# MLP matmuls of two transformer layers as three float32r products of split operands, with weights streamed through a ring

## The chip, the cores and the metric

One core of a Trainium2 chip runs the whole kernel in one launch. The metric is the device time in microseconds (us), the median of several executions. The engines are TensorE (PE, with its weight loads shown apart as PEld), VectorE (DVE), ScalarE (ACT), GpSimd (POOL), and SyncE (SP), whose queue issues every DMA of this kernel.

## The reference

Two layers run one after the other on `x` (2 batches, 1024 tokens, 256 features) and a context of 154 tokens per batch, with 16 heads of 16 features. All numbers are float32.

```python
# layer 0
h = ln(x);  x = x + attn(rope(h wq), rope(h wk), h wv, causal=True) wo
h = ln(x);  x = x + attn(rope(h wq), rope(y wk), y wv, causal=False) wo
h = ln(x);  x = x + gelu_tanh(h @ fc1_w + fc1_b) @ fc2_w + fc2_b        # 256 -> 1024 -> 256
# layer 1: queries from x, keys and values from the context
h = ln(attn(x Wq.T, y Wk.T, y Wv.T, causal mask) + x)
out = gelu(h @ W1.T + b1) @ W2.T + b2 + h                               # 256 -> 1024 -> 256
```

Biases are left out of the attention lines. The two MLPs are what the change touches.

## The kernel before

The 2048 tokens are cut into four chunks of 512 (`c` = 0 to 3; the last is `LAST`). For each chunk the kernel goes through: layer norm and projections (`prologue`), causal self-attention (`sa`), cross-attention of layer 0 (`ca`), MLP of layer 0, cross-attention of layer 1 (`la`), layer norm, MLP of layer 1, store. Every one of these is cut into small steps: `("max", ...)` computes a tile of scores and its row maximum, `("row", ...)` turns the maxima and places them as an extra row of the queries by two DMAs, `("exp", ...)` computes scores again and exponentiates, `("pv", ...)` multiplies with the values, `("place", ...)` scatters a projection's parts by six DMAs, `("stats", ...)` and `("tr", ...)` are a layer norm and its transposes.

An MLP (`mlp(l, c)`) is 8 pairs of steps. `up` m multiplies the chunk's 256 features with 128 of the 1024 hidden columns: two matmuls of 512 columns into the one bank `ps_misc`. ScalarE applies gelu from there into `hid` (two slots). `down` m multiplies this piece with 128 rows of the second weight: four matmuls of 256 columns which are summed over all 8 pairs in the two banks `ps_exp`. `res` adds the sums to the residual. The order is up 0, up 1, down 0, up 2, down 1, and so on. There are 8 MLPs, so 64 pairs. All MLP weights lie in SBUF as `w_up` and `w_down` (4 MB in all): those of layer 0 are loaded at the start, those of layer 1 at the step `late`.

The order of all steps is one list, `ORDER`. `order()` makes it with a planner at build time: ten threads of steps, a table `COST` of assumed durations, and priorities; it takes at each turn the step that could start on the PE first. Each engine then walks the same list and does its part of every step, in order. Since the sums of an MLP occupy `ps_exp`, the planner lets no `exp` step stand between the first `up` and the `res` of an MLP; `max` steps may stand there. Since every engine is in order, a wait in one step holds up all later steps of that engine. GpSimd has little to do: the third part of each projection (L1248), eight instructions per chunk for the output of the last layer norm (`lnout`, L1255), and some setup.

The steps of the prediction are in these places: `up` and `down` on PE at L835 and L852, gelu at L1191, `max` at L889 and L891 on PE and at L1114 on DVE, the SP queue at L622 to L709.

## Time and profile before

| | |
|---|---|
| median of 3 runs | 1119.23 us |
| lowest, highest | 1112.74, 1123.27 us |
| span of the profiled execution | 1118.3 us |
| PE busy | 936.4 us (84%) |
| DVE busy | 582.5 us (52%) |
| ACT busy | 419.9 us (38%) |
| POOL busy | 73.3 us (7%) |
| HBM read, written | 13.32 MB, 2.10 MB |

The profiled execution has a span of 1118.3 us from its first to its last instruction. No time of its own is given beside that; the span is 0.9 us under the median of the runs. Busy times are unions of the records. A PE record contains the drain of the array, so two matmuls that follow each other overlap in the records, and the spacing of their starts is what a matmul costs in a stream.

### The profile page before, as it was taken

What the parts mean: (1) busy time and instruction counts of PE and PEld (TensorE: products, weight loads), DVE (VectorE), ACT (ScalarE), POOL (GpSimd) and SP (SyncE); (2) the same over time, 40 slices, a digit from 0 to 9 for tenths busy, and PEclk for the clock granted to TensorE, in tenths of its full rate; (3) what the DMA queues carried; (4) which work ended last, traced back from release to release, by engine and by line L of the source; (5) the groups of instructions that cost most, each with busy time, mean ns of one, the idle gap of its engine ahead of it and who ended that gap; (6) DMA issues with size and microseconds to landing.
All of it is one profiled execution on the core that took longest, in us unless ns stands there. A gap on an engine that the chain in (4) does not pass through costs nothing.

```text
span 1118.3 us, 13782 instructions
## 1 busy us (share of the span) xinstructions
PE 936.4 (84%) x5180; PEld 456.9 (41%) x5180; DVE 582.5 (52%) x1347; ACT 419.9 (38%) x822; POOL 73.3 (7%) x83
## 2 busy tenths in 40 slices
PE   3888864899988898888989867999887888987898
PEld 1433322345443353434445324633233454442365
DVE  5555637784667704488545675665125504415500
ACT  1133331342355625353422431167763323343421
POOL 2102000000000200000000001000000000000210
PEclk9988886799999999988999897999998999998999
DMA  7805462202132100645020401013004004022000
GB/s 275 102 1 73 75 139 43 24 2 27 23 38 30 29 1 20 94 51 66 1 30 1 57 13 17 10 40 48 1 20 57 2 1 57 2 37 22 1 19 19
DMA packets 47013, 43.85 MB, mean 39 GB/s; under 512 B 13510, under 2 KB 44386, under 8 KB 46434
## 3 DMA queue, kind: packets, MB, share of 16 engines
q1 hardware_dynamic: 46948, 42.98, 24.0%
q8 instruction: 42, 0.69, 0.3%
q14 instruction: 23, 0.19, 0.1%
HBM read 13.32 MB, written 2.10 MB: 14 GB/s over the span
## 4 chain that ended last, share of the span: by engine, by line
PE 57%; DVE 17%; DMA 10%; ACT 8%; SPq 5%; issue 4%; ACTq 0%; DVEq 0%
PE ps_exp L852 10%; PE ps_o L964 10%; PE ps_misc L835 10%; PE ps_max L889 8%; ACT probs L1200 5%; DVE mcol L1114 5%; SPq L695 4%; PE ps_exp L922 4%; DMA QA<-part 4%; PE ps_chain L814 3%; PE ps_chain L822 3%; DVE swap L1028 2%; DMA QC<-part 2%; PE ps_exp L927 2%; PE ps_chain L787 2%
## 5 line engine op out<-in xcount | busy, mean ns | idle before, releaser
L1114 DVE TENSOR_REDUCE mcol<-ps_max 128x3 f32<-128x462 f32 (+5 forms) x496 | 292.2, 626 | 181.9 <-PE ps_max L891 106.1
L1200 ACT ACTIVATE probs<-ps_exp 128x512 f32<-128x512 f32 (+3 forms) x544 | 261.1, 523 | 242.0 <-PE ps_exp L925 87.0
L889 PE MATMUL ps_max<-KA,QA 96*128 96x512 bf16 (+3 forms) x384 | 117.9, 359 | 55.3 <-DVE mcol L1114 24.4
L922 PE MATMUL ps_exp<-QA,KA 98*128 98x512 bf16 (+3 forms) x384 | 120.4, 350 | 26.1 <-ACT probs L1200 18.3
L835 PE MATMUL ps_misc<-hT,w_up 128*128 128x512 f32 x256 | 125.7, 615 | 7.2 <-ACT hid L1191 2.2
L852 PE MATMUL ps_exp<-w_down,hid 128*128 128x256 f32 x512 | 128.2, 388 | 0.0
L1191 ACT ACTIVATE hid<-ps_misc,col 128x512 f32<-128x512 f32 x64 | 44.0, 687 | 200.4 <-PE ps_misc L835 200.4
L852 PEld LDWEIGHTS ps_exp<-w_down,hid 128*128 128x128 f32 x512 | 94.5, 190 | 29.7 <-issue 15.5
L1248 POOL TENSOR_TENSOR part<-rot,part 128x512 bf16<-128x512 f32 (+1 forms) x36 | 40.8, 1133 | 923.2 <-DVE part L1038 923.2
L889 PEld LDWEIGHTS ps_max<-KA,QA 96*128 96x128 bf16 x384 | 39.2, 104 | 123.1 <-DVE mcol L1114 63.6
L964 PE MATMUL ps_o<-probs,V 128*17 128x512 f32 (+3 forms) x768 | 85.1, 517 | 3.2 <-ACT probs L1200 2.3
L922 PEld LDWEIGHTS ps_exp<-QA,KA 98*128 98x128 bf16 x384 | 36.9, 101 | 115.4 <-ACT probs L1200 88.5
L1028 DVE TENSOR_TENSOR swap<-rot,sinT 64x512 f32<-64x512 f32 (+1 forms) x56 | 36.9, 659 | 59.0 <-ACT rot L1173 48.2
L835 PEld LDWEIGHTS ps_misc<-hT,w_up 128*128 128x128 f32 x256 | 47.9, 195 | 47.3 <-issue 41.3
L891 PE MATMUL ps_max<-mask,idb 128*128 128x128 bf16 (+1 forms) x320 | 65.8, 234 | 0.0
L889 PE MATMUL ps_max<-KC,QC 96*128 96x154 bf16 x384 | 53.1, 255 | 10.3 <-DMA QC<-part 5.1
L925 PE MATMUL ps_exp<-mask,idb 128*128 128x128 bf16 x256 | 56.9, 234 | 0.0
L1054 DVE TENSOR_TENSOR xb<-xb,ps_exp 128x512 f32<-128x512 f32 x16 | 10.6, 682 | 85.3 <-PE ps_exp L852 85.3
L1173 ACT ACTIVATE rot<-ps_chain,col 128x512 f32<-128x512 f32 (+1 forms) x36 | 24.1, 668 | 76.1 <-PE ps_chain L814 68.1
L889 PEld LDWEIGHTS ps_max<-KC,QC 96*128 96x128 bf16 x384 | 32.3, 106 | 41.8 <-DVE mcol L1114 24.1
L1157 ACT ACTIVATE hT<-ps_chain,col 128x256 f32<-128x256 f32 x64 | 31.3, 565 | 48.0 <-PE ps_chain L787 47.9
L964 PE MATMUL ps_o<-probs,VA 128*17 128x512 f32 x256 | 36.7, 647 | 14.0 <-ACT osb L1207 13.5
(109 smaller groups left out, 986.6 us busy)
## 6 DMA issues: line engine op xcount, KB each, us to landing
QA<-part SPq DMA_DIRECT2D x72, 128.0 KB, 5.1
QC<-part SPq DMA_DIRECT2D x72, 128.0 KB, 5.2
KA<-part SPq DMA_DIRECT2D x48, 128.0 KB, 5.2
xb<-in_x SPq DMA_DIRECT2D x8, 512.0 KB, 6.1
out<-xb SPq DMA_DIRECT2D x4, 512.0 KB, 3.0
KC<-part SPq DMA_DIRECT2D x24, 77.0 KB, 3.1
w_up<-in_fc SPq DMA_DIRECT2D x1, 1024.0 KB, 7.0
w_down<-in_fc SPq DMA_DIRECT2D x1, 1024.0 KB, 8.2
```

What stands on the lines that cost most here:

```text
L695: sp.dma_start(dst, part[:, n % 2, i, :]).then_inc(s_put[key][f], 16)
L835: mm = pe.matmul(bank[:, :], w_up[l][:, t, m * P:(m + 1) * P], hT_of("up", c)[:, t, :], start=(t == 0), stop=(t == KT - 1))
L852: mm = pe.matmul(dst, hid[:, m % 2, t * P:(t + 1) * P], w_down[l][:, m, :], start=False, stop=(m == NM - 1), skip_group_check=True)
L889: mm = pe.matmul(dst, q, kk, start=True, stop=not causal)
L891: mm = pe.matmul(bank[:, at0 + a0:at0 + a0 + w0], idb[:, :], mk, start=False, stop=True)
L922: mm = pe.matmul(bank[:, q0:CH], KA[:, g // NT, hh, (g % NT) * P:(g % NT + 1) * P], QA[:, hh, q0:CH], start=True, stop=(r < 0))
L925: mm = pe.matmul(bank[:, q0:q0 + P], idb[:, :], maskt, start=False, stop=True)
L964: mm = pe.matmul(ps_o[p0:p0 + HD + 1, q0:CH], v, pr, start=first, stop=last, skip_group_check=True)
L1028: ins = dve.tensor_tensor(w[lo:lo + 64, a0:a0 + wd], r[hi:hi + 64, a0:a0 + wd], sinT[hi:hi + 64, t0:t0 + wd], ALU.mult)
L1114: dve.tensor_reduce(dst, src, AX.X, ALU.max).then_inc(s_max_done, 1)
L1191: act.activation(hid[:, m % 2, :], ps_misc[:, :], (ACT.Gelu_apprx_tanh, ACT.Gelu)[l], bias=c0(("fc1_b", "l1_b1")[l], m)).then_inc(s_misc_f ...
L1200: act.activation(probs[:, n % 2, h, q0:CH], ps_exp[exp_nth[s] % 2][:, q0:CH], ACT.Exp).then_inc(s_exp_done, 1)
```

## The change

Each operand of the MLP matmuls is split into a rounded part and the rest (high and low), and each product is made of three matmuls in the type float32r: high with low, low with high, high with high (`PRODUCTS`). So `up` has six matmuls of 512 columns in place of two in float32, and `down` has twelve of 256 columns in place of four.

**Weights.** At the start 16 `split` steps bring one pair's weights (256 KB) each into `stage`, GpSimd rounds them and subtracts (two instructions), and SP writes both parts (512 KB) to a scratch in DRAM. A step `refill` then loads the first six pairs into the ring `wm`, and each `down` is followed by the load of the pair six further on. The 4 MB of resident weights are gone.

**Activations.** After the transposes of ln3 and ln4 come two `round` steps: DVE rounds half of the chunk into `hTr`, GpSimd computes the rest. After each gelu DVE copies `hidf` to `hidh` rounded, and GpSimd writes the rest to `hidl`; `down` waits for that. These buffers lie in the memory of `probs`, so the gelu of the first pair waits for all earlier `pv` steps, and the planner starts an MLP only when none is open.

**Order.** The table `COST` is changed and the planner places everything anew. The places that the prediction speaks of follow.

PE in the MLP of layer 1 for chunk 1, third and fourth pair. Names: `w_up`, `w_down` are the weights before, `wm` the ring, `ps_max` the score tiles. Before:

```order
L835 MATMUL ps_misc<-hT,w_up 128x512 x2
L889 MATMUL ps_max<-KA,QA 128x512 x2
L852 MATMUL ps_exp<-w_down,hid 128x256 x4
L889 MATMUL ps_max<-KA,QA 128x512
L891 MATMUL ps_max<-mask,idb 128x128
L889 MATMUL ps_max<-KA,QA 128x512
L891 MATMUL ps_max<-mask,idb 128x128
L835 MATMUL ps_misc<-hT,w_up 128x512 x2
```

Now:

```order
L994 MATMUL ps_misc<-idf,mcol 16x128
L921 MATMUL ps_misc<-hTr,wm 128x512 x6
L941 MATMUL ps_exp<-wm,hidh 128x256
L941 MATMUL ps_exp<-wm,hidl 128x256
L941 MATMUL ps_exp<-wm,hidh 128x256 x2
L941 MATMUL ps_exp<-wm,hidl 128x256
```

Most `max` steps have left this MLP. It had 34 between its first `up` and its `res` and has 5; over the 8 MLPs the number falls from 99 to 60 (20, 4, 27, 34, 6, 8, 0, 0 before in the order in which they run; 22, 6, 13, 5, 0, 14, 0, 0 now).

GpSimd at the end of the program, last two MLPs of layer 1. Before, `lnout` was all that stood there:

```order
L1255 TENSOR_TENSOR xb<-a_ctx,g4b 128x256 x4
L1255 TENSOR_TENSOR xb<-xb,g4b 128x256 x4
L1255 TENSOR_TENSOR xb<-a_sa,g4b 128x256 x4
L1255 TENSOR_TENSOR xb<-xb,g4b 128x256 x4
L444 UNCONDITIONAL_BRANCH
```

Now:

```order
L1380 TENSOR_TENSOR hTr<-hT,hTr 128x2x256 x2
L1387 TENSOR_TENSOR xb<-a_sa,g4b 128x256 x4
L1387 TENSOR_TENSOR xb<-xb,g4b 128x256 x4
L1374 TENSOR_TENSOR hidl<-hidf,hidh 128x512 x8
L1380 TENSOR_TENSOR hTr<-hT,hTr 128x2x256 x2
L1387 TENSOR_TENSOR xb<-a_ctx,g4b 128x256 x4
L1387 TENSOR_TENSOR xb<-xb,g4b 128x256 x4
L1374 TENSOR_TENSOR hidl<-hidf,hidh 128x512 x8
```

The eight instructions of `lnout` stand before the first rest of the hidden piece (`hidl`), and the rounding of the second MLP's input stands behind the last `hidl` of the first. Chunk 3 now goes before chunk 2 here.

SP after the first projections. Before, the row of the first four heads was next:

```order
L695 DMA QA<-part 16x8x512 x6
L695 DMA KA<-part 16x8x512 x12
L658 DMA xb<-in_x 128x4x256
L702 DMA QA<-mrow 1x16x128 x4
L695 DMA QA<-part 16x8x512 x6
```

Now:

```order
L783 DMA QA<-part 16x8x512 x6
L783 DMA KA<-part 16x8x512 x12
L727 DMA xb<-in_x 128x4x256
L740 DMA split_w<-wm 128x1024
L744 DMA stage<-in_mlpw 128x512
```

Eight such pairs of a scratch write and a stage load (the first is shown) stand before the first row, four more before the second, and three more before the next projection is placed. On GpSimd the two instructions of each split stand after the first three projection parts.

The diff, cut to its core:

```diff
+PRODUCTS = ((0, 1), (1, 0), (0, 0))
...
+NWM = 6
+WSTEP = KT * P + E
+SPLIT_SLOTS = 4
...
+def rounded(name, c):
+    s = norm(name, c)
+    return s[:3] + [("round", name, c, 0)] + s[3:] + [("round", name, c, 1)]
...
-    return (post_norm("sa", "ln2", c) + cross("ca", c) + out_norm("ca", "ln3", c)
+    return (post_norm("sa", "ln2", c) + cross("ca", c) + out_norm("ca", "ln3", c)[:-2] + rounded("ln3", c)[2:]
             + mlp(0, c) + [("tr", "x3", c, g) for g in range(NT // 2)] + cross("la", c)
-            + [("addatt", c, g) for g in range(NT // 2)] + norm("ln4", c) + [("lnout", c)] + mlp(1, c)
+            + [("addatt", c, g) for g in range(NT // 2)] + rounded("ln4", c) + [("lnout", c)] + mlp(1, c)
...
+def splits():
+    return [("split", l, m) for l in (1, 0) for m in range(NM)] + [("refill",)]
...
-    "up": (("pe", 1.8), ("act", 0.6)), "down": (("pe", 1.78),), "res": (("dve", 0.65),),
+    "up": (("pe", 1.32), ("act", 0.65), ("dve", 0.4), ("pool", 1.15)), "down": (("pe", 1.35),),
+    "round": (("dve", 0.4), ("pool", 1.15)), "split": (("pool", 2.3), ("dma", 1.3)), "res": (("dve", 0.65),),
...
+            w += [("round", ("ln3", "ln4")[s[1]], s[2], g) for g in range(NT // 2)]
+            w.append(("refill",))
...
+        if holder not in (None, i) and k == "round":
+            return None
+        if k == "up" and s[3] == 0 and (part_group or len(pvs) < exp_groups):
...
+        stage = alias("stage", [P, 2, WSTEP], F32, addr["hTr"], 0)
+        hidf = alias("hidf", [P, 2, CH], F32, addr["probs"], 0)
+        hidh = alias("hidh", [P, 3, CH], F32R, addr["probs"], 2 * CH * 4)
+        hidl = alias("hidl", [P, 3, CH], F32R, addr["probs"], 5 * CH * 4)
...
+        def after_down(eng, n):
+            l, m = divmod(n, NM)
+            if m == NM - 1:
+                eng.wait_ge(s_sum_ready, (l + 1) * NT // 2)
+            else:
+                eng.wait_ge(s_down, l * (NM - 1) + m + 1)
...
+                elif k == "split":
+                    _, l, m = s
+                    n = nth[s] - 1
+                    sp.wait_ge(s_split, n + 1)
+                    sp.dma_start(split_w[l * NM + m], wm[:, n % SPLIT_SLOTS, :, :].rearrange("p a n -> p (a n)").bitcast(F32)
+                                 ).then_inc(s_wput[n % SPLIT_SLOTS], 16)
+                    if n + 2 < len(SPLITS):
+                        l, m = SPLITS[n + 2][1:]
+                        sp.dma_start(stage[:, n % 2, :], mlpw[l * NM + m]).then_inc(s_stage[n % 2], 16)
...
+                elif k == "refill":
                     after_chain(sp, ("ctxk", 1, KT - 1))
-                    sp.dma_start(w_up[1][:, :, :], fcw[2]).then_inc(s_wlate, 16)
-                    sp.dma_start(w_down[1][:, :, :], fcw[3]).then_inc(s_wlate, 16)
+                    for i in range(SPLIT_SLOTS):
+                        sp.wait_ge(s_wput[i], 16 * len(SPLITS) // SPLIT_SLOTS)
+                    for n in range(NWM):
+                        _, l, _, m = ups[n]
+                        sp.dma_start(wm[:, n, :, :].rearrange("p a n -> p (a n)").bitcast(F32), split_w[l * NM + m]
+                                     ).then_inc(s_wload[n], 16)
+                elif k == "down" and nth[s] - 1 + NWM < len(ups):
+                    n = nth[s] - 1 + NWM
+                    _, l, _, m = ups[n]
+                    after_down(sp, n - NWM)
+                    sp.dma_start(wm[:, n % NWM, :, :].rearrange("p a n -> p (a n)").bitcast(F32), split_w[l * NM + m]
+                                 ).then_inc(s_wload[n % NWM], 16)
...
                 elif k == "up":
                     _, l, c, m = s
-                    for g in range(NT // 2):
-                        after_chain(pe, ("tr", ("ln3", "ln4")[l], c, g))
-                    if l:
-                        once("wlate", s_wlate, 32)
-                    elif m == 0:
-                        once("wrest", s_wrest, 16 * 7)
+                    n = nth[s] - 1
+                    pe.wait_ge(s_round, nth[("round", ("ln3", "ln4")[l], c, NT // 2 - 1)])
+                    pe.wait_ge(s_wload[n % NWM], 16 * (n // NWM + 1))
                     bank = misc_bank(s)
-                    for t in range(KT):
-                        mm = pe.matmul(bank[:, :], w_up[l][:, t, m * P:(m + 1) * P], hT_of("up", c)[:, t, :],
-                                       start=(t == 0), stop=(t == KT - 1))
+                    for i, (a, b) in enumerate(PRODUCTS):
+                        for t in range(KT):
+                            mm = pe.matmul(bank[:, :], wm[:, n % NWM, a, t * P:(t + 1) * P], hTr[:, b, t, :],
+                                           start=(i == 0 and t == 0), stop=(i == 2 and t == KT - 1))
                     mm.then_inc(s_misc_ready, 1)
...
-                    after_misc(pe, ("up", l, c, m))
+                    n = nth[s] - 1
+                    pe.wait_ge(s_hl, n + 1)
                     for t in range(NT):
                         dst = ps_exp[t // 2][:, (t % 2) * E:(t % 2 + 1) * E]
                         if m == 0:
                             add_bias(dst, ("fc2_b", "l1_b2")[l], start=(t % 2 == 0))
-                        mm = pe.matmul(dst, hid[:, m % 2, t * P:(t + 1) * P], w_down[l][:, m, :],
-                                       start=False, stop=(m == NM - 1), skip_group_check=True)
+                        for i, (a, b) in enumerate(PRODUCTS):
+                            hid = (hidh, hidl)[a]
+                            mm = pe.matmul(dst, hid[:, n % 3, t * P:(t + 1) * P], wm[:, n % NWM, b, KT * P:WSTEP],
+                                           start=False, stop=(m == NM - 1 and i == 2), skip_group_check=True)
                         if m == NM - 1 and t % 2:
                             mm.then_inc(s_sum_ready, 1)
+                        elif m < NM - 1 and t == NT - 1:
+                            mm.then_inc(s_down, 1)
...
+                elif k == "up":
+                    n = nth[s] - 1
+                    after_misc(dve, s)
+                    if n >= 3:
+                        after_down(dve, n - 3)
+                    dve.tensor_copy(hidh[:, n % 3, :], hidf[:, n % 2, :]).then_inc(s_hh, 1)
+                elif k == "round":
+                    _, what, c, g = s
+                    n = (nth[s] - 1) // 2
+                    after_chain(dve, ("tr", what, c, g))
+                    if n == 0:
+                        dve.wait_ge(s_split, len(SPLITS))
+                    else:
+                        dve.wait_ge(s_misc_ready, misc_use[ups[n * NM - 1]] + 1)
+                    dve.tensor_copy(hTr[:, 0, :, 2 * g * P:(2 * g + 2) * P],
+                                    hT_of(what, c)[:, :, 2 * g * P:(2 * g + 2) * P]).then_inc(s_rh, 1)
...
                     act.wait_ge(s_misc_ready, misc_use[s] + 1)
-                    act.activation(hid[:, m % 2, :], ps_misc[:, :], (ACT.Gelu_apprx_tanh, ACT.Gelu)[l],
+                    n = nth[s] - 1
+                    if m == 0:
+                        act.wait_ge(s_pv, pvs_before[s])
+                    if n >= 2:
+                        act.wait_ge(s_hl, n - 1)
+                    act.activation(hidf[:, n % 2, :], ps_misc[:, :], (ACT.Gelu_apprx_tanh, ACT.Gelu)[l],
...
+                elif k == "split":
+                    n = nth[s] - 1
+                    i = n % SPLIT_SLOTS
+                    pool.wait_ge(s_stage[n % 2], 16 * (n // 2 + 1))
+                    if n >= SPLIT_SLOTS:
+                        pool.wait_ge(s_wput[i], 16 * (n // SPLIT_SLOTS))
+                    link(pool.tensor_copy(wm[:, i, 0, :], stage[:, n % 2, :]))
+                    pool.tensor_tensor(wm[:, i, 1, :], stage[:, n % 2, :], wm[:, i, 0, :].bitcast(F32),
+                                       ALU.subtract).then_inc(s_split, 1)
+                elif k == "up":
+                    n = nth[s] - 1
+                    pool.wait_ge(s_hh, n + 1)
+                    pool.tensor_tensor(hidl[:, n % 3, :], hidf[:, n % 2, :], hidh[:, n % 3, :].bitcast(F32),
+                                       ALU.subtract).then_inc(s_hl, 1)
+                elif k == "round":
+                    _, what, c, g = s
+                    pool.wait_ge(s_rh, nth[s])
+                    tok = slice(2 * g * P, (2 * g + 2) * P)
+                    pool.tensor_tensor(hTr[:, 1, :, tok], hT_of(what, c)[:, :, tok],
+                                       hTr[:, 0, :, tok].bitcast(F32), ALU.subtract).then_inc(s_round, 1)
```

## Rows read from the trace of the kernel before

**Rows 1.** The page: busy tenths and granted clock in 40 slices of the span.

```profile
PE   3888864899988898888989867999887888987898
DVE  5555637784667704488545675665125504415500
PEclk9988886799999999988999897999998999998999
```

**Rows 2.** The chain that ended last: its share of the span by line.

```profile
PE ps_exp L852 10%; PE ps_o L964 10%; PE ps_misc L835 10%; PE ps_max L889 8%; ACT probs L1200 5%; DVE mcol L1114 5%; SPq L695 4%; PE ps_exp L922 4%; DMA QA<-part 4%; PE ps_chain L814 3%; PE ps_chain L822 3%; DVE swap L1028 2%; DMA QC<-part 2%; PE ps_exp L927 2%; PE ps_chain L787 2%
```

**Rows 3.** Stretches cut at the MLPs (from, to, length, busy by engine, clock, DMA).

```profile
core 0: us, PE busy (x) PEld busy (x) DVE busy (x) ACT busy (x) POOL busy (x), PEclk, DMA share, GB/s
...
390.60:424.50 33.90, 32.27 (x122) 19.14 (x120) 4.38 (x9) 7.32 (x11) 1.29 (x2) 1.00 0.00 1
...
606.40:681.50 75.10, 55.49 (x368) 25.80 (x369) 53.71 (x119) 28.41 (x58) 8.32 (x10) 0.85 0.27 33
681.50:725.20 43.70, 42.48 (x176) 24.98 (x174) 23.83 (x42) 6.59 (x10) 1.06 (x2) 0.95 0.00 1
...
1049.40:1114.90 65.50, 62.10 (x212) 37.94 (x212) 9.95 (x32) 14.63 (x22) 6.17 (x9) 0.97 0.03 9
```

**Rows 4.** Timeline, one pair without other work: start, length, engine, line, count.

```profile
1071.63 1.88 PE L835 MATMUL ps_misc<-hT,w_up 128*128 128x512 f32 x4
...
1073.35 1.89 PE L852 MATMUL ps_exp<-w_down,hid 128*128 128x256 f32 x8
...
1073.55 0.69 ACT L1191 ACTIVATE hid<-ps_misc,col 128x512 f32<-128x512 f32 x1 [2.76 <-PE ps_misc L835]
...
1075.08 0.59 PE L835 MATMUL ps_misc<-hT,w_up 128*128 128x512 f32 x1
```

**Rows 5.** Timeline of PE: float32 transposes of 128 columns between other matmuls.

```profile
1063.87 1.04 PE L787 MATMUL ps_chain<-idf,a_sa 128*128 128x128 f32 x8
1064.74 0.59 PE L835 MATMUL ps_misc<-hT,w_up 128*128 128x512 f32 x1
```

**Rows 6.** Timeline of an MLP with score tiles between its steps.

```profile
697.36 0.60 PE L889 MATMUL ps_max<-KA,QA 96*128 96x512 bf16 x2
697.78 1.29 DVE L1114 TENSOR_REDUCE mcol<-ps_max 128x1 f32<-128x512 f32 x2 [1.20 <-PE ps_max L889]
697.80 1.88 PE L835 MATMUL ps_misc<-hT,w_up 128*128 128x512 f32 x4
```

**Rows 7.** Groups by form: operations like those that are added.

```profile
L1035 DVE CAST part<-rot 128x512 bf16<-128x512 f32 x32 | 13.7, 427 | 27.2 <-ACT rot L1173 26.4
L1248 POOL TENSOR_TENSOR part<-rot,part 128x512 bf16<-128x512 f32 x32 | 37.7, 1179 | 896.2 <-DVE part L1038 896.2
L1255 POOL TENSOR_TENSOR xb<-xb,g4b 128x256 f32<-128x256 f32 x16 | 11.1, 724 | 0.3
L1222 POOL TENSOR_SCALAR w_ca_wq<-w_ca_wq 128x512 f32<-128x512 f32 x1 | 1.5, 1503 | 0.1
L1114 DVE TENSOR_REDUCE mcol<-ps_max 128x1 f32<-128x512 f32 x192 | 125.9, 685 | 87.1 <-PE ps_max L891 48.3 <-PE ps_max L889 38.0
```

**Rows 8.** Timeline at the end: `lnout` on GpSimd, then the last additions and the store.

```profile
1060.77 2.77 POOL L1255 TENSOR_TENSOR xb<-a_sa,g4b 128x256 f32<-128x256 f32 x4 [10.76 <-DVE a_sa L1096]
...
1063.62 2.78 POOL L1255 TENSOR_TENSOR xb<-xb,g4b 128x256 f32<-128x256 f32 x4
...
1113.31 0.69 DVE L1054 TENSOR_TENSOR xb<-xb,ps_exp 128x512 f32<-128x512 f32 x1 [28.74 <-PE ps_exp L852]
1114.18 0.69 DVE L1054 TENSOR_TENSOR xb<-xb,ps_exp 128x512 f32<-128x512 f32 x1 [0.18 <-PE ps_exp L852]
```

**Rows 9.** Timeline of the start: SP's queue, GpSimd's third projection part.

```profile
39.90 1.15 POOL L1248 TENSOR_TENSOR part<-rot,part 128x512 bf16<-128x512 f32 x1 [5.79 <-DVE part L1038]
42.51 0.60 SPq L658 DMA_DIRECT2D xb<-in_x  x1
67.28 11.80 SPq L702 DMA_DIRECT2D QA<-mrow  x4
83.03 3.81 SPq L695 DMA_DIRECT2D QA<-part  x6
```

**Rows 10.** Timeline: who waited at 91.6 and at 169.5 us.

```profile
91.61 0.23 PE L889 MATMUL ps_max<-KA,QA 96*128 96x128 bf16 x1 [0.20 <-DMA QA<-part]
...
169.50 0.69 DVE L1054 TENSOR_TENSOR xb<-xb,ps_chain 128x512 f32<-128x512 f32 x1 [13.14 <-DMA xb<-in_x]
```

**Rows 11.** DMA issues: count, size of one, median us from issue to landing.

```profile
QA<-part SPq DMA_DIRECT2D x72, 128.0 KB, 5.1
...
xb<-in_x SPq DMA_DIRECT2D x8, 512.0 KB, 6.1
out<-xb SPq DMA_DIRECT2D x4, 512.0 KB, 3.0
...
w_up<-in_l1w SPq DMA_DIRECT2D x1, 1024.0 KB, 5.5
...
w_ca_wo<-in_ca_wo SPq DMA_DIRECT2D x1, 256.0 KB, 3.9
```

92 lines of the change are left out of this document (65 added, 27 removed).

## The prediction, made before the changed kernel ran

> **What bounds the kernel now.** I read the page first. PE is 80 to 90% busy in nearly every slice, DVE up to 80% in the first half and idle in stretches of the second [rows 1]. The chain that ended last has L835 and L852, the MLP matmuls, with 10% of the span each [rows 2]. 20% of 1118.3 us is 224 us, and 64 pairs of an `up` and a `down` at 3.45 us each (below) are 221 us: so the whole matmul stream of the MLPs lies on the chain, and a shorter stream can shorten the run.
>
> The stretches say how the MLPs run [rows 3]. The MLP of layer 1 for chunk 0 takes 33.9 us with PE busy 32.3 and the clock at 1.00: PE alone is its limit. The one for chunk 1 takes 43.7 us with 42.5 of PE, because 34 score tiles stand in it; DVE has 23.8 us there and follows easily. The last two take 65.5 us with nothing else to run. The stretch before the MLP of chunk 1 is another kind: 75.1 us with only 55.5 of PE and 53.7 of DVE. Outside the MLPs PE waits for others.
>
> **The stream.** In a bare pair the first `up` record starts at 1071.63, the first `down` at 1073.35, the next `up` at 1075.08 [rows 4]: 1.72 us for `up`, 1.73 for `down`, 3.45 together. One float32 matmul is two records; four records of 512 columns take 1.72, so one matmul takes 0.86. A bfloat16 matmul of 512 columns takes 0.22 (two records in 0.60 with the second one's drain of 0.38) [rows 6]. No row has float32r. The bounds of its price are these two, 0.22 and 0.86, a factor of four apart with no value between them in any row. I take the lower one for streaming: float32's price is four times bfloat16's to the percent, which looks like four products of half-width parts, and a type whose operand is one rounded part has one. The Trainium skill, FP8 and Floating Point Precision, section TensorE Precision Notes, says this of the array: true float32 takes four passes, and reduced float32 is read and cut to its native width, which makes one. By that page the sum would be the same as mine.
>
> `up` is then 6 x 0.216 = 1.30 us. In `down` each matmul has new weights of 4 bytes and only 256 columns (0.11). The nearest row is the eight float32 transposes: each loads 128 new columns and streams 128, and they take 1064.74 - 1063.87 = 0.87, 0.109 each [rows 5], twice what 128 columns stream in. So a load costs about 0.11 and lies beside the stream. With 256 columns both are 0.11, and `down` is 12 x 0.11 = 1.32. A pair is 2.62 in place of 3.45, and 64 pairs give **-53 us**. If loads did not overlap, this would be otherwise (rival 3).
>
> **The chain inside a pair.** `down` m used to need gelu m. Now it needs gelu, a DVE copy and a GpSimd subtraction. Counted from the next PE record after `up` m: 0.20 to the start of gelu, 0.69 gelu [rows 4], 0.43 the copy (CAST, 427 ns), about 1.25 the subtraction (1179 ns with one bfloat16 operand; two float32 operands of 256 take 724) [rows 7], and some 0.27 for three handovers: **L = 2.8 us**. Meanwhile PE has `down` m-1 and `up` m+1, 2.62 us. Where L is the longer, each second step waits and a pair settles at (L + 2.62)/2 = 2.71. Score tiles between steps cover this, so it costs 0.09 in the 32 pairs of chunks 2 and 3 at most: **+2**. With a row maximum (0.69 us, [rows 7]) ahead of the copy, L is 3.5 and the price 14.
>
> **Start and end of each MLP.** `down` 0 has only `up` 1 (1.30) before it, so PE waits 1.5; `down` 7 has only `down` 6, again 1.5. Before, gelu was shorter than either. 3 us in about four MLPs without cover: **+12**. Before `up` 0 come the two `round` steps, of which the second is exposed: 0.43 on DVE and 1.25 on GpSimd and handovers, 2 us in four MLPs: **+8**. In the last pair of MLPs this is worst. The second one's rounding waits on DVE for the `res` steps of the first and then runs twice on GpSimd, about 4 us in which PE has nothing; and `lnout`, 5.6 us of GpSimd [rows 8], stands between the rounding and the first `hidl`, so that `down` 0 comes at 5.6 + 1.3 after `up` 0 starts in place of 4.1. That is 2.8 for each of the two: **+6**. The 4 us are in the +8. So the last two MLPs, 65.5 us now, gain hardly anything: -13 in the stream, +6 for ends, +6 for rounding and +6 for `lnout`.
>
> **The start.** GpSimd begins the splits after its third projection part, at 41.1 us [rows 9]. One split is a copy and a subtraction; no row has a float32 copy there, and a TENSOR_SCALAR of the size took 1.50, a TENSOR_TENSOR 1.18 [rows 7], so one split is 2.4 to 2.9. `stage` has two slots: split n+2 needs the load that SP issues after the write of split n. 0.5 us for issuing the write, then 3.9 us to landing (256 KB with others ahead) [rows 11], then 2.6 for the split: 7.1 for two, 3.55 each, unless the 512 KB write ahead (3.0, as the store) adds itself, then 5. Split 8 ends at 43.7 + 7 x 3.55 = 68.5, against 67.28 when SP issues the first row [rows 9]: nearly nothing. SP passes the 15th at 93.4 and only then places the next projection, which started at 83.03. PE took up the first tile that needs it at 91.61 with 0.20 us of waiting [rows 9, 10], so a placement 10 to 12 us later is felt. The planner put some 3 us of other steps ahead: **+8**, with 0 and +27 (5 us a split) as ends.
>
> Against this stands a wait that goes. The reload of `xb` was issued at 159.38 and used at 169.50, after 13.14 us of idle DVE [rows 10], behind 2 MB of layer-1 weights; its median is 6.1 [rows 11]. Now the ring's 3 MB come behind it: **-5**, at most -6.
>
> **The placing of score tiles.** 39 of the 99 tiles leave the MLPs. In there each cost PE 0.22 to 0.28; outside it costs DVE 0.69 [rows 7]. Where PE waits anyway the move gives back 39 x 0.28 = 11 us; where DVE is the limit, as in the 75.1 us before the MLP of chunk 1 [rows 3], it costs 39 x (0.65 - 0.28) = 14. Both occur: the MLP of chunk 1 goes from 43.7 to about 26 us, and the stretch before it grows by its tiles. I take **-3**.
>
> **More work for DVE and DMA.** 64 copies and 16 roundings are 80 x 0.43 = 34 us of DVE, nearly all in MLPs where it has half its time free; I cost them at nothing beyond L. That cover is thin where a projection's rope (four or five instructions of 0.4 to 0.7 us) stands ahead of a copy; five projections now lie inside MLPs and one did. DMA carries 40 MB more (4 in, 8 out, 32 back, less 4 of old loads). A pair's 512 KB every 2.7 us is 190 GB/s, and the ring is six pairs deep, 16 us, so no `up` should wait for it. But SP is one queue and its placements (5.1 us each, [rows 11]) now queue behind 512 KB loads: **+3** for both, 0 to +10.
>
> **Sum.** -53 + 2 + 12 + 8 + 6 + 8 - 5 - 3 + 3 = -22 us against the profiled 1118.3: 1096. The median of the runs is 0.9 above that span, so the forecast is **1097 us**.
>
> **Rivals.**
>
> 1. *The stream's gain comes nearly whole.* The ends are covered by other chunks' steps, the moved tiles fall where PE waits (-11), the start costs nothing. -53 + 0 + 6 + 5 + 4 + 0 - 5 - 11 + 2 = -52: 1067 us. For it: PE is busy 55.5 of 75.1 us in [rows 3], so there is room. Against it: the last two MLPs have no cover.
>
> 2. *The chain through three engines becomes the bound* (slower). A pair costs (L + 2.62)/2. The other terms add up to +29, without the +2 for L. So if all 64 pairs run at L, the run is no faster from 3.45 - 29/64 = 3.0 us a pair on, which is L = 3.4, about what one row maximum ahead of the copy gives. At L = 3.9 (a maximum and a slow subtraction) a pair is 3.26: -12 + 29 = +17, 1136 us. For it: DVE and GpSimd are in order and DVE's maxima stand between `up` steps. Against it: the tiles that delay the copy also fill PE.
>
> 3. *Weight loads do not overlap with the matmuls of float32r* (slower). Then each of the 18 matmuls of a pair costs 0.11 more: 2.62 + 2.0 = 4.6 us, 64 x 1.15 = +74, with the others 1220 us. The trace speaks against it: the transposes run at 0.109, where 0.107 for the load and 0.053 for the stream would be 0.16 one after the other [rows 5]. The Trainium skill, TensorE: Matmul & The Clock Gate, Part 3, The mechanism, says that weight loads overlap with matmuls in flight only where the row group differs, which would make this rival true; here float32 loads of the same rows overlap, and the measurement decides.
>
> 4. *The start eats the rest.* At 5 us a split the projection comes 27 us late, and the sum is -3: 1116 us, no change.
>
> **How the numbers follow.** A difference of 1% (11 us) is what a measurement of this kernel can tell. The forecast (1080 to 1112) gets 0.50, rival 1 0.15, rival 2 0.15, rival 3 0.03, rival 4 and mixtures near zero 0.17. Faster, under 1108: nearly all of the forecast's case (0.45) and rival 1, 0.60. Within 1%: the rest of the forecast's case and rival 4, 0.21. Slower: rivals 2 and 3, 0.18, and a little of 4, 0.19. The range of 8 in 10 runs from rival 1's end with 4 us more, 1063, to rival 2's 1136.
>
> **What would show it.** L921 and L941 records starting 0.216 and 0.11 apart (wrong if 0.21 for L941). In the last MLP a pair every 2.7 us; a higher value gives L. PE idle 4 us between the last two MLPs, and some 3 more before the first `down` after `lnout`. SP's first `QA<-mrow` near 69 us and the next `QA<-part` near 94. The wait for `xb<-in_x` near 160 us shrinking to about 3. The MLP of chunk 1, layer 1, at 26 us. The forecast is wrong if the stretches between MLPs grow together by more than 20 us, or if `up` waits for the ring.

## The result: 3.5% slower, and the profile after

The changed kernel takes 1157.03 us (median of 4 runs, 1154.93 to 1158.85), the kernel before beside it 1117.68 (4 runs): a ratio of 1.035, 95% interval 1.030 to 1.039. The forecast was 1097, faster; the time lies outside the range of 1063 to 1136. The profiled execution spans 1157.1 us against 1118.3, so 39 us are to be found.

The page of the changed kernel first: PE and its granted clock in 40 slices, the chain that ended last, and the groups that answer to [rows 1, 2, 7] (busy us, mean ns | idle before, releaser).

```profile
PE   3886875898998977989878786979896898876678
PEclk9897777799999988999989697989997799979588
...
PE ps_o L1055 10%; PE ps_exp L941 7%; PE ps_max L980 6%; PE ps_misc L921 6%; DVE mcol L1221 5%; ACT probs L1312 4%; PE ps_exp L1013 4%; SPq L783 4%; PE ps_chain L902 3%; PE ps_chain L910 3%; DMA QC<-part 3%; DMA QA<-part 2%; DMA stage<-in_mlpw 2%; PE ps_exp L1018 2%; PE ps_chain L875 2%
...
L921 PE MATMUL ps_misc<-hTr,wm 128*128 128x512 f32 x384 | 113.4, 435 | 17.0 <-POOL hTr L1380 12.6
L941 PE MATMUL ps_exp<-wm,hidh 128*128 128x256 f32 x512 | 117.5, 304 | 11.7 <-POOL hidl L1374 11.7
...
L1374 POOL TENSOR_TENSOR hidl<-hidf,hidh 128x512 fp32r<-128x512 f32 x64 | 82.4, 1289 | 170.6 <-DVE hidh L1151 170.6
...
L1151 DVE CAST hidh<-hidf 128x512 fp32r<-128x512 f32 x64 | 31.9, 500 | 146.0 <-ACT hidf L1303 145.9
...
wm<-split_w SPq DMA_DIRECT2D x64, 512.0 KB, 3.3
```

The stream did shrink: L921 and L941 hold 13% of the chain where L835 and L852 held 20% [rows 2]. What is new is idle PE with GpSimd's name on it, 12.6 us before `up` and 11.7 before `down` (3.7 more stand before the bias matmuls that open `down` 0), and a lower clock: 0.89 on average against 0.93. PE is busy 935.7 us, as before (936.4), though its stream is shorter. The ring is no bound; no group of PE names `wm<-split_w`. The eight MLPs together take 278.2 us against 283.6, so all the rest of the program has grown by 44 us.

A bare pair, late in the MLP that runs last but one (start, length, line, count), as [rows 4]:

```profile
1098.38 1.55 PE L921 MATMUL ps_misc<-hTr,wm 128*128 128x512 f32 x6
1099.76 0.34 PE L941 MATMUL ps_exp<-wm,hidh 128*128 128x256 f32 x1
...
1101.25 1.55 PE L921 MATMUL ps_misc<-hTr,wm 128*128 128x512 f32 x6
```

`up` takes 1.38 (six matmuls, 0.23 each), `down` 1.49 (twelve, 0.12 each), a pair 2.87, and 2.82 to 2.87 elsewhere. A float32 matmul of 512 columns took 0.86 [rows 4], so this one costs little over a quarter, and the load of its 4-byte weights is hidden. So rival 3 is dead. The Trainium skill, TensorE: Matmul & The Clock Gate, Part 3, The mechanism, says in its list that loads overlap with matmuls in flight only when the row group differs, though its text also names a background weight buffer as a second way; here they overlap on the same rows, `down` at 0.12 a matmul. The Trainium skill, FP8 and Floating Point Precision, TensorE Precision Notes, gives float32 four passes and reduced float32 a read that is cut to the native width; the trace agrees with one pass for it. But 2.85 is not 2.62.

The end of the run, the changed kernel's stretches from the last step of attention on: from, to, length, then busy time of each engine, clock, DMA.

```profile
1065.80:1082.50 16.70, 3.10 (x13) 2.30 (x13) 12.81 (x54) 4.24 (x7) 2.66 (x3) 0.61 0.00 0
1082.50:1115.60 33.10, 30.69 (x150) 24.40 (x151) 4.46 (x9) 5.51 (x8) 15.87 (x16) 0.78 0.34 112
1119.70:1153.00 33.30, 29.97 (x148) 23.61 (x148) 4.91 (x10) 5.51 (x8) 15.88 (x16) 0.80 0.10 35
```

For 16.7 us PE has 3.1 us of work, while DVE does 12.8: two chunks are normalized one behind the other. Then two MLPs take 33 us each at a clock of 0.78 and 0.80, where the bare MLP of the kernel before took 30.4 at 1.00. Three things stand there in one place: an order, waits at the edges, and half clock behind them. The chain shows the edge (start, length, what):

```profile
1079.84 2.60 POOL hTr L1380 x2
1082.43 2.77 POOL xb L1387 x4
1085.27 2.96 POOL xb L1387 x4
1088.23 1.24 POOL hidl L1374
...
1094.69 2.42 PE ps_misc L921 x6
```

Rounding, then all of `lnout`, then the rest of the first gelu, all on GpSimd, before the first `down`; and an `up` at 1094.69 that takes 2.42 us for the six matmuls that take 1.39 a pair later: the granted clock was still 0.5 until 1096.8, while PE had its work again from 1089.6 on.

### The profile page after: what moved, and what is told of

Same layout as the page of the kernel before. It is cut to its first block, busy times and chain, and to the rows that moved or that the text cites. A ratio compares the mean times of both kernels' runs of the same rounds, so it can differ in the third digit from the quotient of the medians.

```text
span 1157.1 us, 14983 instructions
## 1 busy us (share of the span) xinstructions
PE 935.7 (81%) x5564; PEld 489.9 (42%) x5564; DVE 624.7 (54%) x1427; ACT 419.1 (36%) x820; POOL 207.2 (18%) x195
## 4 chain that ended last, share of the span: by engine, by line
PE 49%; DVE 18%; DMA 11%; ACT 7%; POOL 5%; SPq 5%; issue 4%; POOLq 0%; DVEq 0%; ACTq 0%
PE ps_o L1055 10%; PE ps_exp L941 7%; PE ps_max L980 6%; PE ps_misc L921 6%; DVE mcol L1221 5%; ACT probs L1312 4%; PE ps_exp L1013 4%; SPq L783 4%; PE ps_chain L902 3%; PE ps_chain L910 3%; DMA QC<-part 3%; DMA QA<-part 2%; DMA stage<-in_mlpw 2%; PE ps_exp L1018 2%; PE ps_chain L875 2%
## 5 line engine op out<-in xcount | busy, mean ns | idle before, releaser
L1221 DVE TENSOR_REDUCE mcol<-ps_max 128x1 f32<-128x512 f32 (+5 forms) x496 | 291.0, 625 | 102.5 <-PE ps_max L982 54.0
L980 PE MATMUL ps_max<-KA,QA 96*128 96x512 bf16 (+3 forms) x384 | 119.9, 360 | 48.1 <-DVE mcol L1221 34.8
L1013 PE MATMUL ps_exp<-QA,KA 98*128 98x512 bf16 (+3 forms) x384 | 119.4, 347 | 26.8 <-ACT probs L1312 18.8
L921 PE MATMUL ps_misc<-hTr,wm 128*128 128x512 f32 x384 | 113.4, 435 | 17.0 <-POOL hTr L1380 12.6
L941 PE MATMUL ps_exp<-wm,hidh 128*128 128x256 f32 x512 | 117.5, 304 | 11.7 <-POOL hidl L1374 11.7
L1374 POOL TENSOR_TENSOR hidl<-hidf,hidh 128x512 fp32r<-128x512 f32 x64 | 82.4, 1289 | 170.6 <-DVE hidh L1151 170.6
L1303 ACT ACTIVATE hidf<-ps_misc,col 128x512 f32<-128x512 f32 x64 | 44.1, 689 | 186.5 <-PE ps_misc L921 186.5
L1151 DVE CAST hidh<-hidf 128x512 fp32r<-128x512 f32 x64 | 31.9, 500 | 146.0 <-ACT hidf L1303 145.9
L941 PEld LDWEIGHTS ps_exp<-wm,hidh 128*128 128x128 f32 x512 | 88.8, 197 | 24.5 <-POOL hidl L1374 18.2
L921 PEld LDWEIGHTS ps_misc<-hTr,wm 128*128 128x128 f32 x384 | 74.6, 206 | 38.0 <-POOL hTr L1380 13.7
L980 PEld LDWEIGHTS ps_max<-KA,QA 96*128 96x128 bf16 x384 | 37.4, 101 | 125.8 <-DVE mcol L1221 91.9
L1380 POOL TENSOR_TENSOR hTr<-hT,hTr 128x512 fp32r<-128x512 f32 x16 | 20.3, 1272 | 310.0 <-DVE hTr L1160 310.0
L941 PE MATMUL ps_exp<-wm,hidl 128*128 128x256 f32 x256 | 74.1, 289 | 0.0
L980 PE MATMUL ps_max<-KC,QC 96*128 96x154 bf16 x384 | 54.2, 258 | 11.0 <-DMA QC<-part 6.4
```

Source lines behind the costliest of these rows:

```text
L921: mm = pe.matmul(bank[:, :], wm[:, n % NWM, a, t * P:(t + 1) * P], hTr[:, b, t, :], start=(i == 0 and t == 0), stop=(i == 2 and t == KT - 1))
L941: mm = pe.matmul(dst, hid[:, n % 3, t * P:(t + 1) * P], wm[:, n % NWM, b, KT * P:WSTEP], start=False, stop=(m == NM - 1 and i == 2), skip_ ...
L980: mm = pe.matmul(dst, q, kk, start=True, stop=not causal)
L1013: mm = pe.matmul(bank[:, q0:CH], KA[:, g // NT, hh, (g % NT) * P:(g % NT + 1) * P], QA[:, hh, q0:CH], start=True, stop=(r < 0))
L1221: dve.tensor_reduce(dst, src, AX.X, ALU.max).then_inc(s_max_done, 1)
L1303: act.activation(hidf[:, n % 2, :], ps_misc[:, :], (ACT.Gelu_apprx_tanh, ACT.Gelu)[l], bias=c0(("fc1_b", "l1_b1")[l], m)).then_inc(s_misc_ ...
```

## The experiments

Ratios are to the kernel before, run beside each on the same chip (its medians 1117.7 to 1123.7); 0.001 is 1.1 us. In the names, `own` means that the hidden tiles have memory of their own, with a ring of four pairs; `before` and `rule` mean the order of the kernel before, as it is or with the planner's rule on open score groups. lnout_spread, one_split, no_rest and the names with `after` keep the changed kernel's order, after_tail up to its last 174 steps.

```
                          ratio    95% interval       median us
changed kernel            1.0346   1.0301 to 1.0391   1157.0
order_rule_on_f32         0.9831   0.9796 to 0.9866   1103.4
own_hid                   1.0095   1.0055 to 1.0134   1134.7
lnout_spread              1.0274   1.0230 to 1.0318   1152.3
one_split                 1.0199   1.0160 to 1.0239   1144.0
f32_after_order           1.0261   1.0230 to 1.0292   1150.5
own_before_order          1.0162   1.0114 to 1.0210   1138.3
own_rule_order_spread     1.0020   0.9991 to 1.0049   1122.7
no_rest                   1.0092   1.0061 to 1.0124   1131.9
after_tail                1.0231   1.0193 to 1.0269   1146.7
after_warm                1.0291   1.0253 to 1.0329   1153.5
after_dve                 1.0319   1.0281 to 1.0358   1155.8
own_rule_dve              1.0178   1.0133 to 1.0222   1139.8
own_before_no_rest        0.9905   0.9868 to 0.9942   1108.5
own_before_one_product    0.9756   0.9706 to 0.9807   1092.2
f32r_one                  0.8907   0.8851 to 0.8964    996.4
f32r_one_cost             0.9147   0.9076 to 0.9217   1024.2
```

### Four suspects, one alone each

My theory was O, the order: the hidden tiles now lie in the score tiles' memory, and the planner may open an MLP only when no score group is open. Rivals: P, the work at the MLPs' edges (later called W); S, the splits at the start.

```diff
 (order_rule_on_f32: to the planner of the kernel before)
+        if k == "up" and s[3] == 0 and (part_group or len(pvs) < exp_groups):
+            return None
 (own_hid: to the changed kernel)
-NWM = 6
+NWM = 4
-        hidf = alias("hidf", [P, 2, CH], F32, addr["probs"], 0)
+        hid_ = sb("hid", [P, 6, CH])
+        hidf = alias("hidf", [P, 2, CH], F32, addr["hid"], 0)
-        if k == "up" and s[3] == 0 and (part_group or len(pvs) < exp_groups):
-            return None
 (lnout_spread: GpSimd, behind each hidl subtraction of layer 1)
+                        ins = pool.tensor_tensor(x_of(c)[:, t, :], ..., g4b4[:, i, :], (ALU.mult, ALU.add)[i])
 (one_split)
-SPLITS = splits()[:-1]
+SPLITS = splits()[:1]
```

> The kernel before (float32 matmuls, weights resident, gelu tiles of their own) with one rule added to its planner: up 0 of an MLP is not taken while a score group or a pv is open. Theory O (the order is the cause): this rule alone costs most of the loss; the planner's own clock gives 20 to 30 us, so 1138 to 1148 us. Theory P (the third engine in the chain and the work at the edges of the MLPs is the cause): the order costs little, 1113 to 1125 us. Theory S (the splits at the start): the same 1113 to 1125.

> The changed kernel with the MLP's hidden tiles in 12 KB of their own in place of the score tiles' memory, hidh and hidl two deep, the ring four pairs deep in place of six to make room, and the planner's rule on open groups taken out. Theory O: 20 to 30 us come back, 1127 to 1137 us. Theory P: nearly nothing, 1150 to 1158 us. If the ring of four runs dry, up waits for wm and the time does not fall, whatever the order.

> The changed kernel with the eight multiply and add instructions of lnout spread over the MLP, one behind each hidl subtraction, in place of all eight ahead of the first one; the order is the same. Theory P: down 0 comes some 3.5 us earlier in the last two MLPs and up to as much in the two others of layer 1, 7 to 14 us: 1143 to 1150 us. Theory O or S: 1153 to 1157 us.

> The changed kernel with one weight step split in place of sixteen; every load of the ring reads that one step, so the output is not the reference's, and the order is the same. Theory S: the start stretch gets 15 us or more shorter, 1140 us or less. Theories O and P: about 7 us, what the start stretch lost at equal progress of PE (248 us before, 255 after at a fifth of its other work), 1147 to 1153 us.

The first fell clean outside every expectation: with the rule, the float32 kernel is 1.7% **faster**. So the rule is not what costs, and theory O in that form is dead. What is left is stranger: two orders of the same float32 work differ by 19 us, and the planner's own clock, its end of the last step, had them the other way round (1014.7 us for the old, 1017.8 with the rule). own_hid gained 2.5%, in a third order, so by itself it proves nothing on memory. lnout_spread gained 0.7%, 8 us, as expected of the edges; its interval overlaps that of the changed kernel, though the traces differ by 7.5 us too. one_split gained 1.5%, 16 us, more than P allowed and less than S asked: 11 of it are there at a fifth of PE's other work (244.1 us against 255.2).

### Order and work taken apart

The next pair completes a square: old work in the new order, and new work in the old order.

```diff
 (f32_after_order: the kernel before, planned by the changed kernel's planner)
+def order():
+    return [s for s in order_all() if s[0] not in ("split", "refill", "round")]
 (own_before_order: own_hid, planned by the planner of before, new steps put in)
+    for s in order_f32():
+        out.append(s)
+        out += [t for a, t in zip(ANCHORS, SPLITS) if a == s]
+        if s[0] == "tr" and s[1] in ("ln3", "ln4"):
+            held.append(("round", *s[1:]))
+        if s[0] == "up":
+            busy = s[3] < NM - 1
+        if not busy:
+            out += held
+            held = []
```

> The kernel before (float32 matmuls, resident weights, gelu tiles of their own) with the changed kernel's order of all steps, without its split, round and refill steps. It gives the price of the order alone. Theory O (the order is the cause): 15 to 35 us over before, 1138 to 1158 us. Theory W (the work at the MLPs' edges is the cause, and the low clock behind it): within 10 us of before, 1113 to 1133 us.

> The changed kernel's work (three float32r products, splits, ring of four, hidden tiles in their own memory) with the order of the kernel before, the split, round and refill steps put in at the nearest places. It gives the price of the work alone at the old order. Theory O: the stream's 38 to 53 us mostly show, 1075 to 1095 us. Theory W: the edges give the stream back, 1115 to 1135 us.

Both theories hold half. **The order alone costs 2.6%**, 29 us, with not one instruction changed. **The work alone costs 1.6%** at the old order, 18 us, where its stream should have saved 38. Their sum, 4.2%, is near the 3.5% of both together. The square is not quite closed: own_before_order has memory of its own for the hidden tiles and a ring of four, the changed kernel shares memory and has six. That sharing was not run alone; but the changed kernel is only 0.8% over f32_after_order, so it is not what costs most. Neither half of the planner's change makes a slow order by itself: the rule with the old table `COST` gave 0.983, and the new table and steps without the rule gave own_hid's order (1.0095, against 1.0162 for the same work in the old order). The slow order has both.

Where the order loses is read at points where PE has started the same share of its other work (4412 matmul records outside the MLPs in both traces) and has done the same MLPs: f32_after_order is 7 us behind at 45% (489.2 us against 482.5), 20 behind at 70%, 13 at 95%, 28 at the end. So half of it lies in the tail, where the last head of chunk 2 is scored after all of chunk 3. The old order normalizes chunk 3 on DVE inside the MLP of chunk 2, as this row of the kernel before shows; that MLP began at 1049.4:

```profile
1059.31 1.38 DVE L1096 TENSOR_SCALAR a_sa<-xb,mv,nw 128x256 f32<-128x256 f32 x4
```

In the new order the same work stands on the chain (f32_after_order: start, length, what, up to the first `up`, which float32 too has to wait for):

```profile
1063.11 1.32 DVE st L1106 x4
...
1070.41 1.42 DVE st L1106 x4
...
1077.38 1.11 PE ps_chain L823 x4
1078.49 3.43 PE ps_misc L871 x4
```

PE's waits tell a part of the rest. Its waits for normalized rows (`a_ctx`), first in the kernel before, then in f32_after_order (us in total, times, longest):

```profile
PE ps_chain L787 <- DVE a_ctx L1096: 6.7, 2, 6.1
PE ps_chain L823 <- DVE a_ctx L1132: 25.5, 7, 7.4
```

Only the 7.4 of it, and 5.8 for the other chunk's rows (`a_sa`), lie in the tail; the other six are spread over the run. The waits for `mcol` grew from 31.6 to 42.3 us, those for placed queries (`QA<-part`) fell from 30.7 to 19.3.

The work is read from the MLPs alone. The sum line gives the length of the eight together, then each engine's busy time; first the kernel before, then own_before_order, whose MLPs hold the same steps in the same order.

```profile
1049.40:1083.90 34.50, 32.73 (x113) 20.08 (x114) 7.90 (x30) 9.13 (x14) 6.17 (x9) 0.95 0.00 0
1083.70:1114.10 30.40, 29.53 (x101) 18.04 (x99) 1.39 (x3) 5.50 (x8) 0.00 (x0) 1.00 0.05 18
sum 283.60, PE 272.30 PEld 164.36 DVE 81.56 ACT 55.93 POOL 10.73; mean PE 34.04 PEld 20.54 DVE 10.19 ACT 6.99 POOL 1.34
```

```profile
583.70:621.40 37.70, 35.77 (x196) 26.34 (x196) 18.76 (x34) 5.51 (x8) 10.18 (x8) 0.90 0.35 100
...
894.50:926.70 32.20, 29.36 (x166) 23.43 (x166) 8.27 (x20) 5.51 (x8) 10.22 (x8) 0.89 0.34 116
...
1063.30:1100.80 37.50, 29.77 (x160) 24.33 (x160) 14.88 (x39) 7.33 (x12) 24.25 (x26) 0.91 0.29 99
1101.80:1129.10 27.30, 25.10 (x148) 20.54 (x148) 4.10 (x9) 5.51 (x8) 10.30 (x8) 1.00 0.36 116
sum 280.10, PE 250.19 PEld 194.89 DVE 106.56 ACT 46.58 POOL 108.33; mean PE 31.27 PEld 24.36 DVE 13.32 ACT 5.82 POOL 13.54
```

64 pairs at 0.6 us less should have made 284 into 245; it is 280. PE's busy time fell by 22 us, not by 38, and its idle time in the MLPs grew from 11.3 us (283.6 less 272.3) to 29.9. The last MLP alone, without cover and at full clock, gained 3.1 us (27.3 against 30.4) of 4.8. The other seven had clocks of 0.89 to 0.96, where before five of the eight had 1.00.

The rest of the work's loss lies outside, 18 us. The start is 8.3 us longer (261.3 against 253.0, as forecast). And once, ahead of the MLP at 583.7, the rounding stood behind a projection's rotation on DVE and GpSimd; PE waited 7.51 us for it:

```profile
583.71 1.22 PE L918 MATMUL ps_misc<-hTr,wm 128*128 128x512 f32 x2 [7.51 <-POOL hTr L1375]
```

```profile
579.27 0.43 DVE L1126 CAST part<-rot 128x512 bf16<-128x512 f32 x1
579.61 1.71 DVE L1157 CAST hTr<-hT 128x512 fp32r<-128x512 f32 x2
...
581.00 2.66 POOL L1375 TENSOR_TENSOR hTr<-hT,hTr 128x512 fp32r<-128x512 f32 x2
```

### The third engine, and what a wait costs

no_rest and own_before_no_rest leave out the two GpSimd subtractions, in the new and the old order.

```diff
-                    pe.wait_ge(s_hl, n + 1)
+                    pe.wait_ge(s_hh, n + 1)
-                            hid = (hidh, hidl)[a]
+                            hid = hidh
 (and hTr[:, 0] for hTr[:, b], no subtraction behind "up" and "round" on GpSimd)
```

> The changed kernel in its own order, without the GpSimd subtractions behind the gelu and behind the rounding of h: the rounded part stands in the products in place of the rest, as many matmuls as before, so the output lacks the rests' share. Theory W: the chain of three engines costs 1.3 us at either end of eight MLPs, 1.3 to 2.6 in the rounding, up to 3.5 of lnout in some (lnout no longer stands ahead of what down 0 waits for), and the low clock behind the waits: 25 to 45 us, 1115 to 1135 us. Theory O: under 12 us, 1148 us or more.

> own_before_order (the changed work in the order of the kernel before, 1.6% over it) without the two GpSimd subtractions; the rounded part stands in the products in place of the rest, as many matmuls as before. Its eight MLPs take 280 us in the trace where the stream alone would have made 284 into 246. Theory W (the waits for the third engine at the MLPs' edges, and the half clock behind them, give the stream back): 20 to 30 us come back, 0.990 to 0.998 of before, 1108 to 1118 us. If the split at the start and DVE's extra work are what counts: less than 8 us, 1.010 or more.

Both bring back 2.5 to 2.6% (1.0346 to 1.0092, 1.0162 to 0.9905), 29 us, with as many matmuls. That holds the waits, the half clock behind them, and `lnout`, which then no longer stands ahead of `down` 0. The eight MLPs of own_before_no_rest:

```profile
886.50:914.90 28.40, 26.39 (x166) 22.13 (x166) 8.87 (x21) 6.24 (x9) 0.00 (x0) 1.00 0.37 116
...
1076.70:1102.30 25.60, 24.70 (x150) 20.93 (x148) 4.98 (x11) 5.51 (x8) 0.00 (x0) 1.00 0.44 142
sum 258.70, PE 242.35 PEld 191.80 DVE 106.19 ACT 50.00 POOL 7.57; mean PE 30.29 PEld 23.97 DVE 13.27 ACT 6.25 POOL 0.95
```

21.4 of the trace's 26.8 us (1133.2 less 1106.4) come out of the MLPs. The last one is now 25.6 us: eight pairs at 2.85 and 2.8 for its two ends. The one at 886.5 went from 32.2 to 28.4 and its clock from 0.89 to 1.00: with the wait the low clock is gone too. 258.7 is still 13 over 245; the DVE copy is still in the chain, and one of these MLPs ran at a clock of 0.80.

after_warm prices that clock: the changed kernel with matmuls of nothing in PE's waits around the last two MLPs.

```diff
+WARM = {("turn", "la", 2, 3): 20, ("tr", "ln4", 3, 1): 18, ("tr", "ln4", 2, 0): 9, ("up", 1, 3, 1): 15,
+        ("tr", "ln4", 2, 1): 12, ("up", 1, 2, 1): 14}
+                    for _ in range(WARM[s[1]]):
+                        pe.matmul(ps_max[0][:, :], idb[:, :], mask[:, 0:512], start=True, stop=True)
```

> The changed kernel with 88 matmuls of nothing (bfloat16, 512 columns, into a bank that nobody reads) at six places where PE waits before and in the last two MLPs. Theory C (after a wait PE runs at half clock, and that is part of the price): the 14.3 and 13.7 us of low clock inside these MLPs go, 8 to 14 us less than the changed kernel, about 1145 us. Without it (only the waits themselves cost): no change, or 1 to 3 us more, since the matmuls can stand in the way.

```profile
1070.40:1087.20 16.80, 12.05 (x59) 5.65 (x58) 12.83 (x54) 4.24 (x7) 2.69 (x3) 1.00 0.01 1
1087.20:1117.50 30.30, 28.31 (x165) 22.16 (x166) 4.83 (x9) 5.51 (x8) 15.88 (x16) 1.00 0.35 122
1121.60:1151.70 30.10, 28.11 (x162) 21.83 (x162) 4.81 (x9) 5.51 (x8) 15.88 (x16) 1.00 0.11 39
```

Same waits, same order, clock 1.00 in place of 0.61, 0.78 and 0.80: the two MLPs take 30.3 and 30.1 us in place of 33.1 and 33.3. In the traces that is 6.0 us, less than the 8 to 14 expected, and less than half of the 14 that 28.0 us at half clock could cost; the traces as a whole differ by only 1.3 us, since this one was already 4.6 behind at the first filler matmul. The ratio went down by 0.006, also 6 us, but the two intervals overlap, so by the runs alone it would be open. The Trainium skill, TensorE: Matmul & The Clock Gate, HAM oscillation — how this bites in real kernels, says that a wait throttles PE and the work behind it starts at half clock; the trace agrees.

own_before_one_product keeps everything but two of the three products.

```diff
-PRODUCTS = ((0, 1), (1, 0), (0, 0))
+PRODUCTS = ((0, 0),)
```

> own_before_order with one float32r product in place of three, all copies, subtractions, splits and ring loads kept; the output lacks the rests' share. PE's part of a pair falls from 2.85 to 0.95 us. If PE's stream still set the pace of the MLPs: 64 times 1.9, 120 us less. By the chain (gelu, copy, subtraction and handovers, 2.8 us) a pair settles at (2.8 + 0.95)/2 = 1.9 us: 64 times 0.95, 60 us less where nothing else covers, less some for more half clock and for MLPs with score tiles in them: 40 to 65 us less, 1073 to 1100 us.

```profile
1061.30:1083.40 22.10, 15.87 (x52) 9.22 (x52) 3.85 (x9) 5.50 (x8) 10.16 (x8) 0.73 0.42 139
sum 228.40, PE 169.21 PEld 100.14 DVE 106.42 ACT 46.45 POOL 107.19; mean PE 21.15 PEld 12.52 DVE 13.30 ACT 5.81 POOL 13.40
```

Two thirds of the stream gone, 122 us, and the run gains 4.1%, 46 us, within the 40 to 65 expected. The pair itself is slower than the 1.9 us expected, 2.1 over four pairs of this last MLP at full clock, where `down` waits for the subtraction:

```profile
1072.05 0.73 PE L938 MATMUL ps_exp<-wm,hidh 128*128 128x256 f32 x4 [0.53 <-POOL hidl L1369]
...
1080.56 0.74 PE L938 MATMUL ps_exp<-wm,hidh 128*128 128x256 f32 x4 [1.01 <-POOL hidl L1369]
```

So with three products PE's stream (2.85) and the chain of gelu, copy and subtraction (2.8) are of one size, and little of a shorter stream comes through: 46 us of 122.

### Repairs

after_tail gives the changed kernel the old order for its last 174 steps; after_dve and own_rule_dve put the subtractions on DVE; own_rule_order_spread has the order of order_rule_on_f32 and `lnout` spread as above.

```diff
 (after_tail)
+    o = o[:o.index(("res", 0, 3, 1)) + 1]
+    return o + [tuple(...) for s in TAIL.split()]
 (after_dve, own_rule_dve)
+                    dve.wait_ge(s_hh, n + 1)
+                    dve.tensor_tensor(hidl[:, n % 3, :], hidf[:, n % 2, :], hidh[:, n % 3, :].bitcast(F32),
+                                      ALU.subtract).then_inc(s_hl, 1)
```

> The changed kernel with the last 174 steps (all behind the second layer-0 MLP of the last two chunks) in the order that the kernel before has them in; the round steps stand behind their transposes. The last head of chunk 2 is then scored before chunk 3's, so that one chunk's last normalization runs on DVE beside work of PE. Theory O (half of the order's loss sits in this tail: 28.5 us at the end against 13.7 at 95% of PE's other work): 10 to 18 us less than the changed kernel, 2.1 to 2.6% over before, 1143 to 1150 us. If the tail's place in the order is not what costs: within 5 us of the changed kernel.

> The changed kernel with both subtractions (hidl, and the rest of h) on DVE behind the rounding copies, in place of GpSimd. An instruction should take 0.65 us in place of 1.29, one handover less, and lnout no longer stands ahead of down 0. Theory W: most of what leaving the rests out brought (2.5%), 15 to 22 us less than the changed kernel, 1135 to 1143 us. If DVE's time is what counts (80 more instructions, 52 us more of DVE): no gain, 1152 us or more.

> The changed kernel's work with hidden tiles of their own, in the order that ran the float32 kernel 1.7% faster (the planner of before with the one rule), and lnout spread behind the hidl subtractions. If orders and work add up: own_before_order less 19 and less some 8, so 1065 us by theory O and 1090 to 1105 by theory W; the second would be below both kernels too.

> The float32r work with hidden tiles of their own, in the order that ran the float32 kernel 1.7% faster, with both subtractions on DVE; lnout as in the changed kernel, now off the chain. By the sum of what was measured (1.002 with lnout spread, about 1% more for the subtraction): 1105 to 1115 us, below the kernel before and not below 0.983 of it. If DVE's time counts: 1120 us or more.

after_tail gained 1.15%, 13 us: the tail's half of the order's loss, shown on the changed kernel itself. after_dve gained nothing that the runs can tell: 0.3%, within its interval. On DVE the subtraction takes 777 ns (0.65 expected), and the waits for rests fell only from 12.6 and 11.7 us to these:

```profile
L921 PE MATMUL ps_misc<-hTr,wm 128*128 128x512 f32 x384 | 115.2, 440 | 15.1 <-DVE hTr L1167 11.2
L941 PE MATMUL ps_exp<-wm,hidh 128*128 128x256 f32 x512 | 116.5, 302 | 6.4 <-DVE hidl L1153 6.3
```

What DVE does more is ahead of the row maxima: PE's waits for `mcol` (L980) rose from 43.0 us to 48.9. In the better order the same move costs 1.6% (1.0020 to 1.0178; there `lnout` is also back in one piece, on a GpSimd without subtractions), and PE's waits for `mcol` are 46.1 us with the subtractions on DVE against 31.9 without, while those for the rests are 8.9 against 19.0. In both orders GpSimd is no worse a place for them, and in the better one it is the better place. own_rule_order_spread, the best order found with `lnout` spread, brings the whole change to 1.002: no change against the kernel before, and 1.9% over the float32 kernel in that order.

### A version below both

Last, what the stream alone is worth, with nothing around it: the kernel before, the order of order_rule_on_f32, every MLP product as one float32r product.

```diff
+                pool.tensor_copy(up_r[l][:, :, :], w_up[l][:, :, :]).then_inc(s_wr, 1)
+                pool.tensor_copy(down_r[l][:, :, :], w_down[l][:, :, :]).then_inc(s_wr, 1)
-                        mm = pe.matmul(bank[:, :], w_up[l][:, t, m * P:(m + 1) * P], hT_of("up", c)[:, t, :],
+                        mm = pe.matmul(bank[:, :], up_r[l][:, t, m * P:(m + 1) * P], hT_of("up", c)[:, t, :],
 (f32r_one_cost, besides)
-    "up": (("pe", 1.8), ("act", 0.6)), "down": (("pe", 1.78),)
+    "up": (("pe", 0.48), ("act", 0.7)), "down": (("pe", 0.5),)
```

> The kernel before in the order of order_rule_on_f32 with every MLP product as one float32r product: weights stay resident and are rounded in place by four GpSimd copies, ScalarE writes h and the gelu as float32r, nothing is subtracted, split or streamed. PE's part of a pair is 0.95 us in place of 3.45 and no third engine stands in the chain; gelu (0.69 and 0.3 of handovers) makes it about 1.0. Against order_rule_on_f32 (1103): 64 times 2.4, 155 us less if all of it shows, 950 us; if waits and half clock at the edges take back as much as they did with three products, some 50 us of it goes, 1000 us. Either is below both kernels.

> The same with the planner's costs of up and down set to what one product takes (0.48 and 0.50 us of PE), so that it lays out the order anew. If the planner's view of time is good, 5 to 15 us less than f32r_one; orders with the same work have differed by 4% here without the planner seeing it, so anything within 20 us either way would not surprise.

```profile
982.30:997.10 14.80, 12.37 (x54) 8.64 (x52) 1.47 (x3) 5.51 (x8) 0.00 (x0) 0.88 0.10 35
sum 179.10, PE 147.38 PEld 95.14 DVE 85.38 ACT 58.00 POOL 14.98; mean PE 18.42 PEld 11.89 DVE 10.67 ACT 7.25 POOL 1.87
```

996 us, 11% below the kernel before and 9.4% below order_rule_on_f32. Its MLPs take 179 us in place of 284. It is no like for like: the rests' share of each product is left out. A kernel that must keep the full products has order_rule_on_f32 at 0.983. f32r_one_cost, with the planner told the true prices, is 2.7% slower than without: again an order that the planner held for good.

## Why the prediction was wrong, point by point

- **The placing of score tiles, -3.** The step that failed most. I reasoned over 39 tiles that leave the MLPs and took gain and loss as balanced. Measured on unchanged float32 work, the new order costs 28 us in the trace and 2.6% in the runs. The tiles were not the mechanism in the half that I can name: chunk 2's last head had moved behind chunk 3, two normalizations stood in a row on DVE, and after_tail gave 13 us back. I had read the last two MLPs before as having "nothing else to run", but DVE normalized chunk 3 inside the first of them. The other half, 20 us by 70% of the work, 13 at 95%, is located in part, in waits for normalized rows and row maxima; no run isolates it. The sign of being wrong that I had named is there: outside the MLPs the run grew by 44 us, where I had said 20.
- **The stream, -53.** The mechanism held (about a quarter of float32's price, loads hidden); the size did not. A pair is 2.85, not 2.62, since each matmul takes 0.23 and 0.12 where I had 0.216 and 0.11: -38 us. 15 us of the miss.
- **Chain, start and end of each MLP, rounding, lnout: +2, +12, +8, +6.** With the stream these made -25 for the MLPs. At the old order they measured -3.5 inside the MLPs and +7.5 in one wait ahead of one: 29 us off. The waits are not the miss: PE's idle time in the MLPs grew by 18.6 us, with the 7.5 by 26, where +28 was forecast, and from `up` 0 to `down` 0 behind `lnout` it took 7.1 us (1082.49 to 1089.61; 6.9 forecast). The miss is PE's busy time, which fell by 22 us and not by 53: 15 of it is the stream's size, and for the other 16 the candidate is what I left out, half clock. The MLPs' clocks in own_before_order (0.92, 0.90, 0.90, 0.96, 0.89, 0.95, 0.91, 1.00) lose up to 20 us of 280, by (1 - clock) times length, against 5 before: up to +15. That is an upper bound, and not isolated at this order: by the same sum the last two MLPs of the changed kernel lose 14, and after_warm gave 6.0 back. I counted each wait at its length, and never asked what PE's clock does behind it, though [rows 1] showed dips. The chain's length of 2.8 us was right: on the changed kernel's chain 2.54 us lie between a gelu's start and its `down` (1111.36 to 1113.90), and 0.2 before it. The period worked out from it was not: 2.1 us a pair with one product, where 1.9 was expected.
- **A rounding behind a projection** was near what I named (cover "is thin where a projection's rope" stands ahead of a copy) and costed at nothing. It cost 7.5 us once.
- **The start, +8: right.** The stretch grew by 8.3 us at equal order, SP's first row went out at 70.66 (69 forecast) and the late placement at 94.83 (94 forecast). With one split in place of sixteen the run was 16 us shorter; 5 of it came later and are not explained. Against the kernel before, the changed one is 7 behind at a fifth of PE's other work.
- **The reload, -5: right in size.** DVE's wait for `xb` near 160 us is 7.2 in place of 13.14, not the 3 given as a sign.
- **Queue and DMA, +3: open.** No `up` waited for the ring, as forecast. At the old order PE's waits for placed queries are 40.0 us against 30.7, but that holds the start's delay too.
- **The MLP of layer 1 for chunk 1** takes 31.4 us at a clock of 0.95, where 26 was forecast.
- **Rival 2** had the right sign and the nearest time, 1136, with a wrong mechanism: the bare pair, at full clock, stayed at 2.87 us or below. The loss was in edges and order.
- In sum at the old order: forecast -19 from all terms of work (-22 less the -3), measured +15 in the trace; and the order +28 where -3 was forecast. 34 and 31 us, of one size. The two add up to 43 where the trace of both together has 39, so 4 us are an interplay or noise.

## What to carry to other kernels

When a change feeds new costs or a new rule to a planner, the order is a change of its own, as large as the one intended: run the old work in the new order, and the new work in the old one, before explaining anything. Price a wait of PE by its length and by the work behind it that runs at half clock (here 3 us for an MLP of 33). A faster stream on one engine is worth only what the chain across the others leaves, and a step of another engine at a loop's first and last turn is paid in full however well it hides in the middle.

## What the runs showed of the hardware that was not expected

- A float32r matmul of 512 columns takes 0.23 us and one of 256 with new weights 0.12, 7 to 8% over the 0.216 and 0.11 that the bfloat16 and float32 rows had led to.
- PE's clock stayed low after work was back: in the changed kernel's last-but-one MLP the matmuls from 1089.6 on ran at 0.5 until 1096.8. With only one product a pair, PE at 16 us of work in 22, the clock was 0.73 in the MLP itself.
- DVE's rounding copy takes 500 ns on average beside GpSimd's subtractions and 429 with the subtractions on DVE (after_dve). The Trainium skill, Advanced Engine Details and Errata, VectorE Performance Modes, says that DVE's second port is shared with GpSimd and that instructions of the two which need it hinder each other; the trace agrees, at 71 ns an instruction.
- On GpSimd a float32 copy of 512 columns takes 620 ns and a subtraction of the same size 1306, so a split was 1.9 us, not 2.4 to 2.9.
